# A Strassen-Winograd kernel: a ring of eight for the right operand, a new order of the first steps, another bank for the fourth tile, and a last tile in two halves

## The reference

```python
# layer 0: x as (4, 512, 1024), one label for each of the 4; rank 32
x1 = x + x @ W0.T + (x @ A0[label0]) @ B0.T * 0.5
# layer 1: x1 as (8, 256, 1024), one label for each of the 8; rank 16
out = x1 + x1 @ W1.T + b + ((x1 @ A1[label1]) @ B1[label1]) * 2.0
```

## Time and profile before

| | before |
|---|---|
| median of 3 runs | 296.58 us |
| the profiled execution | 296.69 us, of which 295.0 us are the span between its first and last instruction |
| TensorE matmul busy | 288.6 us (98%), 1329 matmuls |
| VectorE busy | 222.5 us (75%), 264 instructions |
| ScalarE busy | 144.0 us (49%), 194 instructions |
| DMA, mean over the span | 99 GB/s |
| granted TensorE clock | full in all 40 slices of the page |

### The profile page before, as it was taken

One profiled execution on the slowest core, in us unless ns is written; L12 is line 12 of the kernel. 1 busy time (PEld: TensorE's weight loads), 2 busy tenths in 40 slices (PEclk: granted clock), 3 DMA queues, 4 the chain that ended last, 5 costly groups with the idle time before them and its releaser, 6 DMA issues.

```text
span 295.0 us, 3665 instructions
## 1 busy us (share of the span) xinstructions
PE 288.6 (98%) x1329; PEld 239.3 (81%) x1329; DVE 222.5 (75%) x264; ACT 144.0 (49%) x194; POOL 2.1 (1%) x13
## 2 busy tenths in 40 slices
PE   6999999999999999999999999999999999999995
PEld 5888888888888888778887878888987888788883
DVE  5578989999899999978585999919286956777500
ACT  5386556534386572717363541636463463505112
POOL 0000000000000000000000000000000000000000
PEclk9999999999999999999999999999999999999999
DMA  7399800222532210124041637250002000012222
GB/s 240 115 313 394 265 11 2 72 71 76 156 111 84 73 38 22 51 93 158 1 142 38 178 107 249 70 218 36 0 2 107 36 2 0 0 71 74 107 107 72
DMA packets 18629, 29.21 MB, mean 99 GB/s; under 512 B 2995, under 2 KB 5427, under 8 KB 18611
## 3 DMA queue, kind: packets, MB, share of 16 engines
q1 hardware_dynamic: 18610, 28.98, 29.5%
HBM read 20.58 MB, written 8.39 MB: 98 GB/s over the span
## 4 chain that ended last, share of the span: by engine, by line
PE 93%; DVE 3%; issue 1%; ACT 1%; ACTq 0%
PE ps L876 92%; DVE w_A L279 2%; PE ps L871 1%; DVE w_B L279 1%; ACT ar0h L231 1%; DVE bstk L654 0%; DVE brl L232 0%; ACT m L378 0%; ACT keep_s L381 0%; ACTq L842 0%; DVE fstk L215 0%; DVE astk L220 0%; DVE ones L216 0%; ACTq L118 0%; ACT brh L231 0%
## 5 line engine op out<-in xcount | busy, mean ns | idle before, releaser
L876 PE MATMUL ps<-brh,ar0h 128*128 128x512 f32 x176 | 69.2, 393 | 0.0
L876 PE MATMUL ps<-brl,ar0h 128*128 128x512 f32 x176 | 69.1, 392 | 0.0
L876 PE MATMUL ps<-brh,ar0l 128*128 128x512 f32 x176 | 68.8, 391 | 0.0
L231 ACT ACTIVATE brh<-w_B 128x1024 fp32r<-128x1024 f32 (+1 forms) x40 | 38.9, 973 | 60.9 <-PE ps L876 57.8
L232 DVE TENSOR_TENSOR brl<-w_B,brh 128x1024 fp32r<-128x1024 f32 (+1 forms) x40 | 44.4, 1113 | 27.9 <-ACT brh L231 27.6
L876 PE MATMUL ps<-brh,ar1h 128*128 128x512 f32 x160 | 62.8, 392 | 0.0
L876 PE MATMUL ps<-brl,ar1h 128*128 128x512 f32 x160 | 62.4, 390 | 0.0
L876 PE MATMUL ps<-brh,ar1l 128*128 128x512 f32 x160 | 62.3, 389 | 0.0
L876 PEld LDWEIGHTS ps<-brh,ar0h 128*128 128x128 f32 x176 | 33.3, 189 | 7.4 <-DVE keep_s L339 0.4
L876 PEld LDWEIGHTS ps<-brl,ar0h 128*128 128x128 f32 x176 | 33.3, 189 | 7.3 <-DVE brl L232 0.7
L876 PEld LDWEIGHTS ps<-brh,ar0l 128*128 128x128 f32 x176 | 33.2, 189 | 7.0
(11 more groups left out here) (113 smaller groups left out, 351.3 us busy)
## 6 DMA issues: line engine op xcount, KB each, us to landing
w_B<-in_x SPq DMA_DIRECT2D x32, 256.0 KB, 3.0
out_z<-keep_s SPq DMA_DIRECT2D x23, 256.0 KB, 2.0
w_B<-in_w SPq DMA_DIRECT2D x16, 256.0 KB, 5.8
w_A<-in_w SPq DMA_DIRECT2D x16, 256.0 KB, 5.7
raw<-in_b SPq DMA_DIRECT2D x64, 32.0 KB, 1.8
out_z<-keep_w SPq DMA_DIRECT2D x8, 256.0 KB, 2.1
raw<-in_a SPq DMA_DIRECT2D x8, 128.0 KB, 2.2
a1raw<-in_a SPq DMA_DIRECT2D x8, 64.0 KB, 1.9
```

What stands on the lines that cost most here:

```text
L231: act(waits + spare, lambda e: e.activation(hi, src, ACT.Copy, scale=scale), h, 0.2 + 0.43 * wide)
L876: ins = eng.matmul(out_ap, lhs, rhs, start=first, stop=False, skip_group_check=True)
```

## The change

```diff
-NB = 6
-NRAW = 3
+NB = 8
+NRAW = 2
 LOAD_RATE = 245.0
-WARM = 9
+WARM = 8
...
                     if job.kb > 8:
                         queue = max(queue, free[n] + 0.7) + job.kb / LOAD_RATE
-                        job.token.end = queue + 0.9
+                        loads += 1
+                        job.token.end = queue + (0.5 if loads < 3 else 1.3)
...
         dve([], lambda e: e.memset(fstk[:, :, :].bitcast(F32), 0.0), tk("fzero"), 0.3)
+        plan.jobs[-1].due = 0.0
...
         transfer([], lambda: [(label_t[:, :], labels)], s_lab, tk("labels"), 1)
-        plan.jobs[-1].due = 3.0
+        plan.jobs[-1].due = 7.0
...
-            turn = (0, 1, 0, 1) if stage == 0 else (1, 3, 1, 3) if p == 2 else (0, 1, 3, 0)
+            turn = (0, 1, 0, 1) if stage == 0 else (1, 3, 1, 3) if p == 2 else (0, 1, 3, 2)
...
         for k in range(4):
+            load_w("B11", k)
             load_w("A11", k)
-            load_w("B11", k)
...
         for k in range(3):
-            for i in range(4):
-                step(0, i, k)
+            for passes in [(one,) for one in PASSES] if k < 2 else [PASSES]:
+                for i in range(4):
+                    step(0, i, k, passes=passes)
...
+        def last_sum():
+            bank = xbank(2, 3)
+            act([tk("z", 2, "21", 3), tk("bias"), tk("stored", 2, "s1", 3, 0, 0)], lambda e: e.activation(
+                keep["s1"][:, 3, last_halves[1]], ps[bank][:, last_halves[1]], ACT.Identity, bias=bias_t[:, 7:8]), tk("last_sum"), 0.45)
+
+        def last_tile(n, spare_bank):
+            s1 = keep["s1"]
+            for half, bank in enumerate((xbank(2, 3), spare_bank)):
+                cols = last_halves[half]
+                for k in range(4):
+                    step(n, 3, k, ("P", n, 3, half) if k == 3 else None, cols=cols, other=spare_bank if half else None,
+                         more=[tk("last_sum")])
+            z = [ps[bank][:, cols] for bank, cols in zip((xbank(2, 3), spare_bank), last_halves)]
+            act([tk("P", n, 3, 0), tk("last_sum")], lambda e: e.activation(
+                s1[:, 3, last_halves[0]], z[0], ACT.Identity, bias=bias_t[:, 7:8]), tk("kept", n, 3, 0), 0.45)
+            dve([tk("P", n, 3, 1), tk("last_sum")], lambda e: e.tensor_tensor(
+                s1[:, 3, last_halves[1]], z[1], s1[:, 3, last_halves[1]], ALU.add), tk("kept", n, 3, 1), 0.45)
+            for half in range(2):
+                store(2, "s1", 3, 0, 1, tk("kept", n, 3, half), last_halves[half])
...
             tile(n + 1, 0)
             if stage == 1:
                 sum_s2_s4(1)
-            tile(n + 1, 1)
+            step(n + 1, 1, 0)
+            step(n + 1, 1, 1)
             low_f(c0, y[2])
+            tile(n + 1, 1, since=2)
             load_a0(c1)
             tile(n + 1, 2)
-            for i in range(4):
-                if i == 3:
+            for two in PAIRS:
+                if two == (2, 3):
                     tile(n + 1, 3)
-                low_b(stage, 0, 0, i, bank_of(n + 1, i), False, ("z", stage, "11", i))
-                kept(n + 1, i, tk("z", stage, "11", i))
+                for i in two:
+                    low_b(stage, 0, 0, i, bank_of(n + 1, i), False, ("z", stage, "11", i))
+                    kept(n + 1, i, tk("z", stage, "11", i))
...
-            for i in range(4):
+            for i in range(3 if last else 4):
                 tile(n + 6, i)
                 low_b(stage, 0, 1, i, xbank(stage, i), False, ("z", stage, "21", i))
-                for half in ((0, 1) if last and i == 3 else (None,)):
-                    kept(n + 6, i, tk("z", stage, "21", i), half)
+                if last and i == 1:
+                    low_b(stage, 0, 1, 3, xbank(stage, 3), False, ("z", stage, "21", 3), [tk("kept", n + 5, 3)])
+                    last_sum()
+                kept(n + 6, i, tk("z", stage, "21", i))
+            if last:
+                last_tile(n + 6, y[0])
```

More of the change, by code:

```diff
@@ L74, in rehearse @@
         free = dict.fromkeys(list(lanes) + ["pe"], 0.0)
-        free["pe"], queue, at_pe = first_matmul, 1.8, 0
+        free["pe"], queue, at_pe, loads = first_matmul, 1.8, 0, 0
         order = {n: [] for n in lanes}
@@ L154, in bass_blocks @@
         dtmp = [sb(f"dtmp{n}", [R, 512], F32, temps) for n in range(3)]
+        ones = sb("ones", [128, 128], F32, temps)
         temps.close()
@@ L157, in bass_blocks @@
         raw = [sb(f"raw{n}", [128, 512], F32) for n in range(NRAW)]
-        ones = sb("ones", [128, 128], F32)
         eye = sb("eye", [128, 128], F32)
@@ L298, in bank_of, with step @@
                 return xbank(stage, i)
-            turn = (0, 1, 0, 1) if stage == 0 else (1, 3, 1, 3) if p == 2 else (0, 1, 3, 0)
+            turn = (0, 1, 0, 1) if stage == 0 else (1, 3, 1, 3) if p == 2 else (0, 1, 3, 2)
             return ybank(stage, turn[i])
-        def step(n, i, k, end=None):
-            p, bank = n % 7, bank_of(n, i)
-            for a, b in PASSES:
+        def step(n, i, k, end=None, passes=PASSES, cols=slice(0, 512), other=None, more=()):
+            p, bank = n % 7, bank_of(n, i) if other is None else other
+            fresh = p < 4 or other is not None
+            for a, b in passes:
                 begins = k == 0 and (a, b) == (0, 0)
@@ L308, in step, with tile @@
                 if begins:
-                    waits = (take(bank) if p < 4 else [tk("kept", n - 4 if p == 4 else n - 1, i)]) + waits
+                    waits = (take(bank) if fresh else [tk("kept", n - 4 if p == 4 else n - 1, i)]) + waits
+                    waits = waits + list(more)
                 last_one = (a, b) == (1, 0)
                 name = end if last_one and end else ("Bk", n, k) if last_one and i == 3 and n else None
-                pe(ps[bank][:, :], ar[n % 2][a][:, i, k, :], b_tile(n, k, b), begins and p < 4, waits, name)
-        def tile(n, i, keep_it=False):
-            for k in range(4):
+                pe(ps[bank][:, cols], ar[n % 2][a][:, i, k, :], b_tile(n, k, b)[:, cols], begins and fresh, waits, name)
+        def tile(n, i, keep_it=False, since=0):
+            for k in range(since, 4):
                 step(n, i, k, ("P", n, i) if k == 3 else None)
@@ L691, in low_f, with low_b @@
             bank_free[bank] = rows_done(1, c)
-        def low_b(stage, c, a, i, bank, start, name):
+        def low_b(stage, c, a, i, bank, start, name, after=()):
             o, chunk = 4 * a + i, 2 * (stage - 1) + c
             pe(ps[bank][:, :], dstk[:, 128 * o:128 * (o + 1)], pstk[c][0][:, :], start,
-               (take(bank) if start else []) + four_done("d", a) + rows_done(0, chunk))
+               (take(bank) if start else list(after)) + four_done("d", a) + rows_done(0, chunk))
             pe(ps[bank][:, :], bstk[c][:, 128 * o:128 * (o + 1)], pstk[c][1][:, :], False,
@@ L747, in run_stage @@
             tile(n + 3, 0)
-            tile(n + 3, 1)
-            low_f(c1, y[2])
             sum_t3(stage)
@@ L752, in run_stage @@
                 sum_s3(1)
+            step(n + 3, 1, 0)
+            step(n + 3, 1, 1)
+            low_f(c1, y[2])
+            tile(n + 3, 1, since=2)
+            if stage == 1:
                 load_a0(c1 + 1)
@@ L755, in run_stage @@
             tile(n + 3, 2)
-            for i in range(4):
-                if i == 3:
+            for two in PAIRS:
+                if two == (2, 3):
                     tile(n + 3, 3)
-                low_b(stage, 1, 0, i, bank_of(n + 3, i), False, ("z", stage, "12", i))
-                kept(n + 3, i, tk("z", stage, "12", i))
+                for i in two:
+                    low_b(stage, 1, 0, i, bank_of(n + 3, i), False, ("z", stage, "12", i))
+                    kept(n + 3, i, tk("z", stage, "12", i))
             split_operands(n + 4)
```

2 lines of the change are left out of this document (1 added, 1 removed).

## The result

The changed kernel took 295.67 us, the median of 22 executions from 293.95 to 297.63; the kernel before took 296.60 on the same chips (296.03 to 297.35, 22 executions). The ratio is 0.9964, with a 95% interval from 0.9946 to 0.9982: 0.36% faster by the ratio, 0.9 us from median to median. I had forecast 294.3 with a range from 293.4 to 295.5, so the sign was right and the median lies just outside the range.

What follows compares the result with a forecast made beforehand. TensorE's stream bounds the kernel (93% of the span), with 2.45 us of hold-ups mid-kernel plus start and tail. -1.65 - 0.70 + 0.3 - 0.3 = -2.35 us from 296.69 gives 294.3, range 293.4 to 295.5.

Steps and rivals of the forecast that it cites:

- The ring: Eight operand slots instead of six let VectorE write operands a product ahead, removing TensorE's mid-kernel hold-ups: 1.65 us less.
- product 8's operand behind product 6 at 105.6: New VectorE wait in the ring of eight, for product 6's end; claimed not to make VectorE late for TensorE.
- The fourth tile's bank and low_f: Fourth tile of products 8, 10, 15, 17 no longer waits for its bank: 0.70 us less; earlier low_f costs nothing.
- the middle: The ring's 1.65 us and the fourth tile's bank's 0.70 us together, out of 2.45 us of hold-ups.
- late rows for `low_f`: Rival: low_f's rows come late at four places, adding 4 d us; 297.1 or more with d 0.7; chance 0.05.
- half the hold-ups coming back: Rival: other late jobs on VectorE or SP return half of the hold-ups, 295.5 us; chance 0.17.
- The tail: After the last matmul's start, last tile in halves: matmuls 0.16 us longer, last store issued 0.3 us sooner.
- The label transfer: Issued behind four weight tiles instead of two, it delays b0s by 0.8 us, bounds 0 and 1.8.
- The sum for the start: From TensorE's start to the first matmul with b0s: -0.48 + 0.8 = +0.3 us, bounds -0.48 and +1.3.
- the room: Time between b0s ready at 17.32 and TensorE taking it at 17.85: 0.48 us, the most the start could gain.
- The start: TensorE's first product 1.0 us sooner; gain 0.48 us at most, since b0s limits it, less any delay of b0s.
- this gap: TensorE waiting ahead of the first matmul with b0s, expected in the profile after, with its weight load near 18.1.

Runs made afterwards that it cites:

- experiment 4: Kernel before with only the label transfer moved behind four weight tiles instead of two: 297.47 us, ratio 1.0036.
- experiment 5: Changed kernel with the label transfer back behind two weight tiles and label 8 read three times instead of once: 295.10 us.
- experiment 6: Changed kernel with the label transfer back behind two weight tiles and label 8 read five times: two executions at 295.66, eight 296.69 to 297.28, two 298.1 us.
- experiment 8: Kernel before with only the changed kernel's start, late label transfer included, and its own last tile: 298.03 us, ratio 1.0053.
- experiment 1: Changed kernel with the label transfer back in third place, behind two weight tiles: 293.50 us, ratio 0.9896.
- experiment 2: Changed kernel with 12 warm-up matmuls instead of 8, label still late: 294.14 us, ratio 0.9911.
- experiment 3: Changed kernel with the early label, and b0raw moved directly behind product 0's eight weight tiles: 292.25 us, ratio 0.9849.

## Why the prediction failed where it did

- *The ring.* Right, cause and size: forecast 1.65, the part alone gave 1.75 (1.6 in the traces, from the first matmul with `b0s` to the last matmul). The place feared most, product 8's operand behind product 6 at 105.6, did not come back as a wait of TensorE.
- *The fourth tile's bank and low_f.* Right: forecast 0.70, the part alone gave 0.6. Together the middle gave 2.5 in the trace and 2.8 in the executions, forecast 2.35. The rivals of late rows for `low_f` and of half the hold-ups coming back appear in no distance of the changed kernel's trace.
- *The tail.* Right: forecast 0.3, measured 0.4 in the traces. The distance of 0.12 that the prediction took from the trace for a half is what the changed kernel has.
- *The label transfer.* Right in cause, and in size for the label alone: delay of the first reading 0.70, forecast 0.8. The Trainium skill (DMA: Bandwidth & Descriptors, Queues, rings and completion order) says that on each DMA engine descriptors are consumed in ring order; that the label would be delayed by the tiles ahead is what I drew from it. The later readings agree, but in part only: in experiment 4 the label was read at 5.30, when the third of the four tiles ahead of it had not landed (6.01). The sum for the start came out at +0.64 instead of +0.3, since the transfer of `b0raw` was 0.66 slower in this execution, for which the forecast had no term, and since the room was 0.70 and not 0.48: I had measured it to the weight load instead of the matmul. Above all, I took one value for something that has a spread. Experiment 4 shows that a late label costs 1.0 us at the median and 2.7 in the slowest execution.
- *The start.* Here is the step that failed, in the prediction's words: "If it rises at the same time, the gain is two matmuls at full speed, 0.5 us; if it comes 1 us sooner, 1.0 or more. But neither counts." It is true that an earlier TensorE gains nothing when `b0s` is the limit. It does not follow that it costs nothing. Product 0 ended 1.2 us sooner, `b0s` came 0.64 later, and the gap of 1.84 us that both make was counted for its length alone. The prediction even names this gap as what the profile would show. What it left out is that in 12 of 22 executions the clock falls, for 1.2 to 1.5 us more where a fall can be compared with none (experiments 5, 6 and 8), and that these are 2.1 us slower as a group, probably since `b0s` was later in them too. The ten executions that kept the clock have a median of 294.5, forecast 294.3. The others lie around 296.6, and the median at 295.67, just beyond a range whose upper end, 295.5, came from cases that all kept the clock.
- *The agreement of the profiled execution* (294.4 against 294.3) is in part luck: the start lost 0.34 us more than the forecast's +0.3, and the middle and the tail gained 0.29 more than theirs.

What stays open is what decides, in one execution and not in the next, whether the clock falls. In executions without a trace the idle stretch can't be read; with a late label its end varies, and with the moment of the clock's first rise its beginning. The share grows with the length of the stretch in the table above, over few executions for some of its rows. Against length alone stand the three slow executions of experiment 4 that kept the clock.

## What to carry to other kernels

An engine that is made ready sooner than its next operand doesn't break even: on TensorE the empty stretch can have a price of its own, so either bring the operand forward as well (here one transfer that needed no label, worth 1.3 us) or leave the start late. When one number of a small transfer's place is moved, follow everything that reads it, down to the first matmul, and expect a spread rather than a value. And read the clock of every execution, not only that of the profiled one: here the one trace with 1.000 looked like a complete success, while the median stood 1.3 us above it.

## What the runs showed of the hardware

- Kernels that idle 1.8 to 2.3 us in their profiled execution (the changed kernel, experiments 5 and 8) had TensorE's granted clock fall to 1.2 GHz in 18 of 37 executions, the one with 3.1 us in 10 of 12, those with 0 to 1.1 us (experiments 1, 2 and 3) in none of 14. In experiment 4 three executions that by the estimate idled 1.8 us or more kept it.
- In the three traces with a mean of 0.994 (experiments 5, 6 and 8) it stayed low for about 3.4 us. Such executions were 1.2 to 1.5 us slower than those of the same kernel with the full clock.
- By the means of the windows it fell not in the empty stretch but behind it, 0.1 us (experiment 6) to 0.5 us (experiments 5 and 8) after TensorE had resumed.
- With one and the same start the clock first rises at different times: in five traces with the start of the kernel before the first fast distance begins at 5.2 to 8.6 us.
- A label transfer of 0.1 KB behind four tiles of 256 KB was read at 5.3 to 6.4 us in five traces, behind two tiles at 4.9 in seven. With it behind four, a kernel that varies by 0.9 us varied by 2.5.
- A transfer of 128 KB (`b0raw`), issued behind the same eight transfers, took 2.1 to 2.8 us to land in eleven traces.
